# Six chained attention stages on one core: outputs of two heads accumulated in the same rows with their denominators beside them, and one score mask made on TensorE

## What is computed

```python
def attention(xq, xkv, wq, wk, wv, wo, mask):
    q, k, v = split_heads(xq @ wq), split_heads(xkv @ wk), split_heads(xkv @ wv)
    scores = einsum('bhqd,bhkd->bhqk', q, k) / sqrt(16)
    # A3 alone: scores = scores * attention_weights
    scores = where(mask, scores, -inf)
    attn = softmax(scores, axis=-1)
    return merge_heads(einsum('bhqk,bhkd->bhqd', attn, v)) @ wo
```

## Time and profile before

| what | value |
|---|---|
| median of 3 runs | 1161.72 us (1161.29 to 1163.68) |
| the profiled execution | 1159.94 us |
| its span | 1157.7 us |
| TensorE clock granted, mean | 0.99 of 2.4 GHz |
| TensorE busy: matmuls / weight loads | 96% / 80% |
| VectorE / ScalarE / GpSimd busy | 73% / 53% / 22% |
| DMA | 45.1 MB, 39 GB/s in the mean, 339 GB/s in the first fortieth |

### The profile page before, as it was taken

How to read it: one execution, slowest core, us unless ns; L and a number is a source line. 1 busy time by engine, 2 the same in 40 slices (tenths; PEclk the granted TensorE clock), 3 DMA queues, 4 the chain that set the end, 5 groups by cost and what they waited for, 6 DMA issues and landing times. The chain is left out here.

```text
span 1157.7 us, 36414 instructions
## 1 busy us (share of the span) xinstructions
PE 1106.9 (96%) x13908; PEld 921.1 (80%) x13908; DVE 841.3 (73%) x3468; ACT 618.6 (53%) x1584; POOL 258.8 (22%) x383
## 2 busy tenths in 40 slices
PE   6999999999999999999999999999999999999886
PEld 5878778888778788878888887888888878787665
DVE  4466987957878687697687777786778685987841
ACT  3644455455555556545556565655556455545453
POOL 0322412203121230222304032320321223121100
PEclk9999999999999999999999999999999999999997
DMA  9600010200111001010010202001010100110000
GB/s 339 246 11 2 2 48 11 84 20 2 28 40 28 39 16 52 2 41 26 16 52 2 66 2 66 2 16 52 16 52 2 52 2 2 52 47 7 2 6 10
DMA packets 21224, 45.11 MB, mean 39 GB/s; under 512 B 2496, under 2 KB 14912, under 8 KB 18112
## 3 DMA queue, kind: packets, MB, share of 16 engines
q1 hardware_dynamic: 19952, 41.36, 10.1%
q10 hardware_dynamic: 1104, 1.44, 0.4%
HBM read 40.70 MB, written 2.10 MB: 37 GB/s over the span
## 5 line engine op out<-in xcount | busy, mean ns | idle before, releaser
L663 POOL TENSOR_TENSOR root<-var_eps,halves 128x1 f32<-128x1 f32 x128 | 76.9, 602 | 609.9 <-DVE var_eps L1171 588.1
L971 ACT ACTIVATE exps_t<-bank 128x512 f32<-128x512 f32 x256 | 135.7, 605 | 34.3 <-PE bank L795 33.8
L1111 DVE CUSTOM_DVE_ANT_0 bank<-bank,bias 128x128 f32<-128x128 f32 x512 | 130.1, 324 | 18.8 <-PE bank L763 18.8
L721 PE MATMUL bank<-x_t,weights_A 128*128 128x128 f32 x1024 | 139.3, 284 | 2.7 <-ACT x_t L931 2.1
L721 PEld LDWEIGHTS bank<-x_t,weights_A 128*128 128x128 f32 x1024 | 127.3, 197 | 12.1 <-ACT x_t L931 4.5
L721 PE MATMUL bank<-x_t,weights_F 128*128 128x128 f32 x1024 | 127.9, 281 | 2.8 <-ACT x_t L931 1.7
L721 PEld LDWEIGHTS bank<-x_t,weights_F 128*128 128x128 f32 x1024 | 121.6, 195 | 9.1 <-ACT x_t L931 3.1
L808 PE MATMUL bank<-exps_t,v_one 128*32 128x128 f32 x3072 | 114.5, 277 | 8.2 <-DVE exps_t L1083 6.1
L714 PE MATMUL bank<-weights_F,exps_t 128*128 128x256 f32 x512 | 121.1, 383 | 0.2 <-DVE neg_max L1111 0.2
L763 PE MATMUL bank<-k_eo,q_t 32*128 32x256 f32 x1536 | 107.7, 396 | 2.6 <-issue 1.7
L1111 DVE DVE_READ_ACCUMULATOR2_ANT neg_max<- 128x1 f32 x768 | 106.5, 139 | 0.1
(11 more groups left out here) (112 smaller groups left out, 1964.8 us busy)
## 6 DMA issues: line engine op xcount, KB each, us to landing
weight<-in_fside SPq DMA_DIRECT2D x16, 1024.0 KB, 4.9
weights_A<-in_weights_A SPq DMA_DIRECT2D x4, 1028.0 KB, 15.3
weights_F<-in_weights_F SPq DMA_DIRECT2D x2, 2054.0 KB, 17.9
drop_raw<-in_drop SPq DMA_DIRECT2D x16, 256.0 KB, 5.3
x_hat<-in_x SPq DMA_DIRECT2D x16, 128.0 KB, 2.5
out<-x_sum SPq DMA_DIRECT2D x16, 128.0 KB, 1.7
ctx_t<-in_ctx_t SPq DMA_DIRECT2D x13, 128.0 KB, 3.0
rows_A<-in_rows_A SPq DMA_DIRECT2D x3, 512.0 KB, 15.4
```

Of the source, the lines that this page charges most:

```text
L663: nc.gpsimd.tensor_tensor(root[x][:], var_eps[x][:], halves[:, e:e + 1], ALU.pow).then_inc(done["root"], 1)
L721: mm = nc.tensor.matmul(dst[:, 128 * f:128 * f + 128], w[:, c, 128 * f:128 * f + 128], tokens_t[:, c, :], start=(c == 0), stop=(c == KC - 1))
L971: nc.scalar.activation(dst, score_bank(x, "ST", s, j)[:], ACT.Exp, scale=DH ** -0.5).then_inc(done["exp"], 1)
L1111: ins = nc.vector.tensor_tensor_reduce(out=heads[:, n, :], in0=heads[:, n, :], in1=mask_bias(x, s), scale=-1.0, scalar=2.0 ** 126, op0=ALU ...
```

## The change

**Outputs.** `v_pairs` holds for every pair of heads 16 values, 16 zeros, 16 values; `ones_pair` the same with ones. The 32 columns that begin at 0 are (values of the even head, zeros), those that begin at 16 (zeros, values of the odd head). Two matmuls, the even head's with `start`, the odd head's with `stop`, so put both heads into the same 32 rows: two column blocks of the bank hold all 256 features of 128 queries, already transposed as `O` needs them. Two more blocks hold the denominators in the same rows, each repeated 16 times, from products with `ones_pair`. VectorE takes the reciprocal of the denominators' 128x256 and multiplies, from PSUM straight into `o_t`. The jobs `oT` and `nT` of TensorE and `o_raw` and `o_t` of ScalarE are gone; the four `PV` jobs of a stage are two.

**The mask of A5.** A5 moves from `ADDED` to `PRELOADED`: TensorE puts the mask into each of the four banks (a bf16 matmul of the 128x128 identity and 512 columns) and the scores are added to it; VectorE's maxima become one reduction for each group.

**The start.** Inputs and contexts of the first six batches, in the order in which TensorE wants them, are divided between the queues of SyncE and ScalarE.

All order tables and bank numbers are new.

```diff
-PRELOADED = {"S": ("A1",), "ST": ()}
-ADDED = ("A0", "A2", "A5")
+PRELOADED = {"S": ("A1", "A5"), "ST": ()}
+ADDED = ("A0", "A2")
...
-        yield from (("PV", s, j) for j in range(GROUPS))
+        yield from (("PV", s, half) for half in range(HALVES))
...
-        yield from (("oT", s), ("nT", s), ("O", s))
+        yield "O", s
...
 TENSOR = """
-12345112112332124001001124551111001122210200010202203000120100001023032323103000230330303010011011201124101000001221
+12345112121224413001001213551102201122200001200430000010230341430330001230031011201120100002102022012201110000210040
...
+FIRST = [beat[0] for beat in TENSOR_ORDER if beat[1:] == ("xT", "A0") and beat[0] < SETS]
...
-        v_one = per_set("v_one", [128, H * VE + 2 * DH - VE])
+        v_pairs = per_set("v_pairs", [128, H // 2, 3, DH])
+        ones_pair = sb("ones_pair", [128, 3, DH])
...
-        o_t = q_t
+        o_t, recip = q_t, x_t
...
             def _(sp):
-                load_x(sp, 0)
+                for x in FIRST[::2]:
+                    load_x(sp, x)
                 load_keys(sp)
-                for x in range(1, SETS):
-                    load_x(sp, x)
                 load_stage(sp, "A1")
-                for x in range(3, SETS):
+                for x in FIRST[::2]:
                     load_ctx(sp, x)
...
+                def of_pair(values, odd):
+                    return values[:, odd:odd + 2, :].rearrange("p a d -> p (a d)")
+
-                def outputs(x, s, j):
+                def outputs(x, s, half):
                     made = "later" if s == "A0" else "keep" if s in ("A2", "A5") else "exp"
-                    pe.wait_ge(done[made], nth(x, made, s, j))
-                    if j == 0:
+                    groups = (2 * half, 2 * half + 1)
+                    pe.wait_ge(done[made], nth(x, made, s, groups[-1]))
+                    if half == 0:
                         pe.wait_ge(values_made(s), nth(x, "v", s))
...
                         free_bank((x, "PV", s, 0))
-                    for n in range(GH):
-                        mm = nc.tensor.matmul(bank((x, "PV", s, 0))[32 * n:32 * n + 32, 128 * j:128 * j + 128], v_one[x][:, VE * head(j, n):VE * head(j, n) + 2 * DH],
-                                              exps_t[EXP_AT[x, s]][:, GH * j + n, :], start=True, stop=True)
+                    for chunk in (half, KC + half):
+                        for odd in range(2):
+                            for at, (j, c) in enumerate((j, c) for j in groups for c in range(KC)):
+                                values = v_pairs[x][:, GROUPS * c + j] if chunk < KC else ones_pair
+                                mm = nc.tensor.matmul(bank((x, "PV", s, 0))[32 * at:32 * at + 32, 128 * chunk:128 * chunk + 128],
+                                                      of_pair(values, odd), exps_t[EXP_AT[x, s]][:, GH * j + 2 * c + odd, :],
+                                                      start=(odd == 0), stop=(odd == 1), skip_group_check=True)
                     mm.then_inc(done["PV"], 1)
...
-                    elif kind == "oT":
-                        pe.wait_ge(done["o_raw"], nth(x, "o_raw", s))
-                        transposes32(dst, o_raw[OUT_AT[x, s]][:].rearrange("p u q -> p (u q)"), GROUPS).then_inc(done["oT"], 1)
-                    elif kind == "nT":
+                    elif kind == "O":
                         pe.wait_ge(done["o_norm"], nth(x, "o_norm", s))
-                        transposes32(dst, o_norm[x], KC).then_inc(done["nT"], 1)
-                    elif kind == "O":
-                        pe.wait_ge(done["o_t"], nth(x, "o_t", s))
                         product(dst[:, 0:D], o_t[x], w_o[s], range(KC), KC).then_inc(done["O"], 1)
...
             def _(act):
                 act.dma_start(weights["A0"][:, 0:half], dram["weights_A0"][:, 0:half]).then_inc(first_loaded, 16)
+                for x in FIRST[1::2]:
+                    load_x(act, x)
                 act.dma_start(weights["A0"][:, half:], dram["weights_A0"][:, half:]).then_inc(stage_loaded["A0"], 16)
-                for x in range(3):
+                for x in FIRST[1::2]:
                     load_ctx(act, x)
...
                 def normalise(x, s):
-                    dve.wait_ge(done["oT"], nth(x, "oT", s))
-                    heads = bank((x, "oT", s))[:].rearrange("p (h e) -> p h e", h=H)
-                    nc.vector.reciprocal(recip[x][:].unsqueeze(2), heads[:, :, DH:DH + 1]).then_inc(recip_made, 1)
+                    dve.wait_ge(done["PV"], nth(x, "PV", s, HALVES - 1))
+                    chunks = bank((x, "PV", s, 0))[:].rearrange("p (c q) -> p c q", c=2 * KC)
+                    nc.vector.reciprocal(recip[x][:], chunks[:, KC:, :]).then_inc(recip_made, 1)
                     dve.wait_ge(recip_made, nth(x, "o_norm", s))
-                    nc.vector.tensor_tensor(o_norm[x].rearrange("p (h d) -> p h d", h=H), heads[:, :, 0:DH],
-                                            recip[x][:].unsqueeze(2).broadcast_to([128, H, DH]), ALU.mult
-                                            ).then_inc(done["o_norm"], 1)
+                    nc.vector.tensor_tensor(o_t[x][:], chunks[:, 0:KC, :], recip[x][:], ALU.mult).then_inc(done["o_norm"], 1)
```

More of the change, by code:

```diff
@@ L21 @@
 SETS = 6
-EXP_BUFFERS, OUT_BUFFERS, PAIR_BUFFERS = 3, 2, 3
-VE = DH + 1
+EXP_BUFFERS, PAIR_BUFFERS = 3, 3
+VP = 3 * DH
+HALVES = 2
 MASKED = -(2.0 ** 100)
@@ L302 @@
         NTH[_beat] = _seen[_beat[1]] = _seen.get(_beat[1], 0) + 1
-TAKEN_BY = {"fold": "folded", "xT": "x_t", "K": "k_eo", "Q": "q_t", "V": "v", "mT": "m_t", "oT": "o_norm", "nT": "o_t", "O": "sum",
-            "Y": "sum", "H": "h_t"}
+TAKEN_BY = {"fold": "folded", "xT": "x_t", "K": "k_eo", "Q": "q_t", "V": "v", "mT": "m_t", "O": "sum", "Y": "sum",
+            "H": "h_t"}
 SCORES = ("S", "ST")
@@ L396, in program @@
         x_t = per_set("x_t", [128, KC, N])
-        o_norm = [t[:].rearrange("p c q -> p (c q)") for t in x_t]
         ctx_t = per_set("ctx_t", [128, KC, N])
@@ L413, in program @@
         exps_t = [sb(f"exps_t{b}", [128, H, N]) for b in range(EXP_BUFFERS)]
-        o_raw = [sb(f"o_raw{b}", [128, GROUPS, N]) for b in range(OUT_BUFFERS)]
-        recip = per_set("recip", [128, H])
-        o_t = q_t
+        o_t, recip = q_t, x_t
         bn = per_set("bn", [128, 6])
@@ L452, in program @@
         stored = sems("stored")
[L453 removed]
+        done = {k: sem(f"done_{k}") for k in ("xT", "K", "Q", "S", "V", "mT", "ST", "shift", "PV", "O",
                                               "H", "Y", "fold")}
[L455 removed]
+        done |= {k: sem(f"done_{k}") for k in ("x_t", "square", "v_copy", "k_copy", "q_t", "m_t", "exp", "h_t")}
         done |= {k: sem(f"done_{k}") for k in ("bias", "pairs", "folded", "k_eo", "v", "times", "lower", "max", "high_low", "keep", "o_norm", "sum",
@@ L525, in slots @@
             return slice(GH * j, GH * j + GH)
-        def heads_of(values):
-            return values[:, 0:H * VE].rearrange("p (h e) -> p h e", h=H)
         def hidden(x, s):
@@ L900, in free_exponentials @@
                     else:
-                        engine.wait_ge(done["PV"], nth(y, "PV", t, GROUPS - 1))
+                        engine.wait_ge(done["PV"], nth(y, "PV", t, HALVES - 1))
             def free_keys(engine, x, s):
@@ L913, in free_values @@
                 if before := stage_before(x, s):
-                    engine.wait_ge(done["PV"], nth(before[0], "PV", before[1], GROUPS - 1))
+                    engine.wait_ge(done["PV"], nth(before[0], "PV", before[1], HALVES - 1))
                 engine.wait_ge(done["V"], nth(x, "V", s))
-                return (heads_of(v_one[x])[:, :, 0:DH], bank((x, "V", s))[:, 0:D].rearrange("p (h d) -> p h d", h=H))
+                return (v_pairs[x][:, :, 0:3:2, :], bank((x, "V", s))[:, 0:D].rearrange("p (g a d) -> p g a d", a=2, d=DH))
             @block.scalar
```

139 lines of the change are left out of this document (58 added, 81 removed).

## The result

The changed kernel takes 1294.17 us, the median of 3 runs (1288.96 to 1296.62), against 1161.72: a ratio of 1.113 [1.107, 1.119], 132 us slower. The forecast was slower, 1192 us; its sign holds, its size does not, and the time lies outside the range of 1158 to 1214. The profiled execution took 1288.96 us, its span 1287.1.

A forecast was written before the change was run, and what follows sets the result against it. TensorE was taken as the bound, with slack elsewhere. Added work of 25.1 us, less 8, 4, 4 and 2 of waits, plus 20 and 3 of new waits, gave +30 us: 1192 us, range 1158 to 1214.

The forecast's parts named there:

- What bounds the kernel: Whole kernel: TensorE, busy 930 of 950 us, is the bound; its added work counts in full, work off ScalarE for nothing.
- Part 1 and 2: TensorE: more output matmul rounds at 0.109 us each, +77.3 us; removed transposes -62.8 us and fewer changes of form -3.3 us.
- Part 3: Stage A5's mask on TensorE: 16 x 4 bf16 matmuls at 0.217 us each, +13.9 us.
- Part 4: Waits that leave: around transposes -8 us, before output matmuls -4, at the start -4, at the tail -2.
- rival (a): VectorE's normalising: the wide reciprocal costs only 0.42 us, like any operation of that width; 1170 us, chance 0.20.
- Part 5: VectorE's normalising: the 128x256 reciprocal takes 1.6 us instead of 0.25, bringing VectorE's busy time to 948 us.
- the other fixed part: Reciprocal estimate: 150 ns, from another one-element operation, as fixed cost; gives 6.3 ns an element and 1.77 us.
- Part 6: Between outputs and projection: too little cover at 26 places, +20 us; VectorE's queue delays, 0 to 20 us, taken as +3.
- the projections' shortfall: TensorE before projections: 26 places with less than 2.3 us of other matmuls; missing cover sums to 24 us.
- Rival (b): VectorE becomes the bound, working no more than 78% of the time in the fixed orders; about 1222 us, chance 0.09.
- Rival (c): TensorE's gaps around the removed transposes vanish, 43 us shed, and the reciprocal is cheap; 1144 us, chance 0.13.
- The sign: Whole kernel: the change makes it slower, chance 0.81, against faster 0.14 and same 0.05.

The follow-up runs named there:

- run 3: The kernel before, in its old orders, with the reciprocals widened from 128x16 to 128x256: 1291.05 us, 1.110 of before.
- run 6: The kernel before plus a wide reciprocal per stage into a spare buffer nobody reads, behind the multiply and off the chain: 1268.66 us, 1.092 of before.
- run 7: The kernel before with ScalarE copying the output bank two and a half times more ahead of the copy that counts: 1288.28 us, 1.109 of before.
- run 1: The changed kernel with its 96 wide reciprocals replaced by copies of the same 128x256, division left out: 1203.03 us, 1.035 of before.
- run 8: The changed kernel with copies for the wide reciprocals and without the products with ones that make the denominators: 1163.06 us, 1.002 of before.
- run 5: The kernel before, in its old orders, with only the mask of A5 moved to TensorE: 1170.74 us, 1.0075 of before.
- run 4: The kernel before with only the change's start, inputs and contexts divided between two queues: 1157.93 us, 0.9967 of before.
- run 9: The changed kernel with all orders, banks and buffers laid out anew by a program for a reciprocal of 1.75 us: 1196.30 us, 1.030 of before.
- run 10: The changed kernel in tables by the same layout program, told 0.42 us for a reciprocal that takes 1.75 on the chip: 1264.55 us, 1.088 of before.
- run 12: The changed kernel in program-made tables laid out for 0.42 us, with copies in place of the wide reciprocals: 1175.47 us, 1.010 of before.
- run 2: The changed kernel with each wide reciprocal made twice: 1519.78 us, 1.308 of before.

## Why the prediction was right and wrong

- **What bounds the kernel.** "A shorter chain of one batch counts only at the tail or where the written order leaves it no cover" was read from TensorE being 98% busy. It is not so the other way round: a busy engine in a fixed order says that all durations fit, not that there is slack. Runs 3, 6 and 7 make it 0.9, 0.6 and 0.9 us of time for each us added to another engine (129 of 144, 107 of 167, 127 of 144), the lower clock of these runs included.
- **Part 1 and 2, rates.** Right. The timeline after has runs of 16 records starting 0.44 us apart, 0.109 us a round. Busy time with the reciprocal out of the way grew 23.8 us (run 1), forecast 25.1. That this work counts in full was not right in the new orders (run 8: 40 of 84 us).
- **Part 3, the mask.** +13.9 forecast; +9 measured (run 5). TensorE's busy time grew by 15.3 us, and VectorE's relief (23 us forecast, 20.9 found), which I gave no worth, is the likely source of the rest.
- **Part 4.** The start is right: -4 and -4 (run 4), first matmul at 5.11 us in the changed kernel. The output matmuls' idle, forecast to fall by 4 us, rose by 33, and 27 of these stand already in run 1. I read the old wait of 8.2 us as the jobs' property; in the tables laid out by the program it is 5.4 to 6.9 us for the same jobs (runs 9, 10 and 12), so it is the order's. These 27 us, where 4 less were forecast, are of the size of the 33 us by which run 1 (1203) lies above rival (a)'s 1170, its own case; that they are the same us is argued, not shown. Waits of the transposes and the tail were not measured apart.
- **Part 5, the reciprocal.** Forecast 1.6, measured 1.75 us; the value worked out from the other fixed part, 1.77, was the nearer. (1752 - 150)/256 is 6.3 ns an element. Put into the step below at its 26 short places, the missing 0.15 us would have added 4 us of waits, not 69. The repeat count of 8 in the Trainium skill, "VectorE: DVE Perf Modes", walkthrough of the 8-slice pipeline, and its 0.96 GHz made it an estimated 2.3 us; the trace does not agree with that size, and the measurement decides. VectorE's busy time: 948 forecast, 955.8 found.
- **Part 6, the step that failed.** "Between 0 and 20 us come through, and I take +3 us." With the projections' shortfall the whole reciprocal stood for 22 us (1192 less rival (a)'s 1170); it cost 91 (the changed kernel against run 1). That makes 69 of the 102 us by which the forecast was short; the other 33 lie in the rest of the change (part 4 above). Two readings were wrong. The shortfall was counted as if VectorE took up a reciprocal as soon as its outputs are made: the projections waited 36 us for the multiply where 24 were summed, and the timeline above has a reciprocal at 1166.75, 2.6 us behind outputs that were ready at 1164.14, since VectorE's order put another batch's values, not yet made, in front of it. And the delay was thought to end at the projection, or to vanish into VectorE's 27% idle; it passes from queue to queue instead. The 22 us would have been near for tables laid out for 1.75 us: there it costs 21 to 30.
- **Rival (b), VectorE as the bound**: 1222, and its test "VectorE over 85%" is not met in any run. Its condition comes nearest to what happened, though: "if the fixed orders let VectorE work no more than 78%". They let it work 74% (955.8 of 1287.1 us), and 74% again in run 2. What it has wrong is the name: the limit is the orders', not VectorE's, as run 9's 80% with the same work shows. Run 1's 69% and run 7's 66%, with 127 us lost, show that it is no fixed share of VectorE either. The warning of the Trainium skill, "TensorEngine Tiling (Array Packing)", PSUM Bottleneck, fits in that the engine that empties the banks is waited for; the trace does not agree that it was short of time, since run 9 does the same work in 98 us less.
- **Rival (c)**, 1144 us, needed holes around the transposes to vanish and a cheap reciprocal. With a copy in its place the new chain took 1203 us in the change's own tables (run 1) and 1175 in run 12's; nothing of (c) shows.
- **The sign** came out right by the forecast's own reason in kind, more TensorE work and a projection that waits for the multiply, not by luck; the size fell short by 102 of the 132 us.

Where the 132 us are: 91 with the reciprocal, in tables not laid out for it; 41 with the rest (run 1), in which are the mask's +9, the start's -4 if they count here as they did alone, and then 36 of output products and waits ahead of them less the transposes. That the change's own tables were laid out for a short reciprocal is inferred: the wide one costs 91 us in them and 89 in run 10's. The tables bear it out: counted roughly, with the rates of part 1 and 2, less than 2.3 us of other batches' matmuls stand between outputs and projection in some 31 of the change's 96 places (26 by the forecast's closer count), in 44 of run 10's and in 6 of run 9's. I did not test it directly.

## What to carry to other kernels

In a kernel whose engines each run one written order, price a job that gets 1 us longer at 0.6 to 0.9 us (what these runs gave) until the order has been laid out anew with the new duration, however idle its engine and whether or not it is on the chain. Measure a new operation's duration in a small run before laying out tables that depend on it. Take changes apart before judging them: the start in this one is worth 4 us by itself (1157.93 us, the fastest version run) and was buried under the rest.

## What the runs showed of the hardware

- A reciprocal of 128x256 from PSUM takes 1752 ns, from SBUF 1742 (run 6), where a copy and a multiply of the same width take 420 (run 1) and 424. For 16 elements it is 251 ns, for one 164.
- Run 2's granted clock of 0.91 was not expected: with TensorE 82% busy, its level was not the upper one of 2.4 GHz throughout, as 0.99 is nearly. Runs 3, 6 and 7 have 0.97 to 0.98 at 88 to 90%, the changed kernel 0.99 at 89% and run 8 0.98 at 91%, so the busy share alone does not tell it. In run 2 TensorE waited up to 6.8 us at a time for VectorE.
- "Busy" hides stalls: the same instructions were busy 1130.7 us in run 1 and 1146.8 in the changed kernel at the same granted clock, 0.990.
